# Folding weights loaded in group 5 and folded in group 11 of a four-block kernel, their sums on GpSimd in the attention

## The reference, cut to what matters

```
x = x + _L0_ffn_ref(_L0_cond_ref(x, itok_B_0_15, L0_cond_weights), L0_ffn_qweight, ...)
x = x + _L1_ffn_ref(_L1_cond_ref(x, L1_cond_Wq, L1_cond_Wk, L1_cond_Wv, L1_cond_Wo, ...), ...)
x = x + _L2_ffn_ref(_L2_cond_ref(x, itok_B_0_15, L2_cond_W, L2_cond_lora_A, L2_cond_lora_B), ...)
x = x + _L3_ffn_ref(_L3_cond_ref(x, itok_B_0_7, ...), ...)
```

```
def _qlora_linear(x, wq, A, B):
    w = jnp.tile(wq, (1, 4))
    base = x @ w.T
    lora = x @ A.T @ B.T
    return base + lora * LORA_SCALING
```

## Time and profile before

| | us |
|---|---|
| median of 3 runs | 2923.24 |
| lowest and highest | 2919.52 and 2926.33 |
| the profiled execution | 2924.63 |
| its span | 2922.9 |
| TensorE busy in the span | 2838.4 |
| first stage (first attention row of TensorE) | 101.67 |

### The profile page before, as it was taken

The page is one execution under the profiler, slowest core; times in us unless marked ns, Lnnn a source line. Parts: engine busy times, 40 slices in busy tenths (PEclk is TensorE's granted clock), DMA queues, the critical chain, the costliest instruction groups (busy, mean ns, idle before and its releaser), DMA issues. The chain is left out here.

```text
span 2922.9 us, 56003 instructions
## 1 busy us (share of the span) xinstructions
PE 2838.4 (97%) x14852; PEld 1935.0 (66%) x14852; DVE 1973.4 (68%) x4703; ACT 1140.2 (39%) x2462; POOL 1523.1 (52%) x1465
## 2 busy tenths in 40 slices
PE   6889999999999999999999999999999999999997
PEld 4566666666666666666666666666666667677775
DVE  5566666666666666566666666666666666677776
ACT  3444444444444444344444444444444444122222
POOL 6566666656666666666666666666666663100000
PEclk9999999999999999999999999999999999999998
DMA  8444444444444444544544444444444446412120
GB/s 306 162 124 122 124 124 124 127 127 127 127 127 127 127 127 127 199 123 123 177 125 127 125 123 120 115 122 125 126 124 119 119 125 196 129 45 58 40 48 15
DMA packets 429458, 363.47 MB, mean 124 GB/s; under 512 B 89094, under 2 KB 369690, under 8 KB 428346
## 3 DMA queue, kind: packets, MB, share of 16 engines
q1 hardware_dynamic: 376346, 184.56, 22.5%
q0 software_dynamic: 49136, 169.56, 18.2%
q10 hardware_dynamic: 3888, 8.24, 0.8%
HBM read 335.14 MB, written 18.61 MB: 121 GB/s over the span
## 5 line engine op out<-in xcount | busy, mean ns | idle before, releaser
L549 DVE CUSTOM_DVE_ANT_0 ps_s<-ps_s,mask 128x544 f32<-128x544 f32 x512 | 374.1, 731 | 537.5 <-PE ps_s L393 524.3
L302 POOL DMA_INDIRECT v_sb<-in_v_rows_w,v_row x504 | 488.4, 969 | 460.0 <-PE ps_oT L421 251.2
L361 PE MATMUL ps_t<-wqkv,xT 128*128 128x512 f32 x1488 | 702.5, 594 | 4.6 <-DMA wqkv<-in_wqkv_w 4.6
L465 ACT ACTIVATE ps_s<-ps_s,nmax 128x544 f32<-128x544 f32 x512 | 352.5, 689 | 868.7 <-DVE nmax L549 868.7
L416 PEld LDWEIGHTS ps_oT<-pT,v_sb 128*128 128x128 f32 x4096 | 528.0, 192 | 189.2 <-issue 176.9
L416 PE MATMUL ps_oT<-pT,v_sb 128*128 128x128 f32 x4096 | 542.8, 276 | 9.5 <-DMA v_sb<-in_v_rows_w,v_row 9.5
L374 PE MATMUL ps_t<-wo,oT 128*128 128x512 f32 x992 | 507.8, 594 | 0.0
L392 PE MATMUL ps_s<-k_sb,qkT 128*128 128x416 f32 x1024 | 445.7, 517 | 6.5 <-PEq L715 4.2
L401 PEld LDWEIGHTS ps_pT<-ident_sb,p_sb 128*128 128x128 f32 x2048 | 256.1, 141 | 270.7 <-issue 246.1
L586 DVE STREAM_TRANSPOSE qkT<-rot 32x640 f32<-32x640 f32 x496 | 414.3, 835 | 14.5
L560 DVE TENSOR_SCALAR p_sb<-ps_s,rinv 128x512 f32<-128x512 f32 x512 | 384.5, 751 | 26.8 <-DVE rinv L557 0.3
(11 more groups left out here) (235 smaller groups left out, 3236.0 us busy)
## 6 DMA issues: line engine op xcount, KB each, us to landing
k_sb<-in_kT SPq DMA_DIRECT2D x2048, 64.0 KB
v_sb<-in_v_rows_w,v_row POOLq DMA_INDIRECT x512
wo<-in_wo_w POOLq DMA_DIRECT2D x2, 4096.0 KB, 14.4
v_new<-v_raw SPq DMA_DIRECT2D x512, 16.0 KB, 1.8
xT<-x1T_scratch POOLq DMA_DIRECT2D x31, 256.0 KB, 5.1
y_scratch<-y_sb SPq DMA_DIRECT2D x31, 256.0 KB
wqkv<-in_wqkv_w SPq DMA_DIRECT2D x6, 1024.0 KB, 12.1
wqkv<-in_wqkv_w POOLq DMA_DIRECT2D x6, 1024.0 KB, 13.9
```

What stands on the lines that cost most here:

```text
L302: e.indirect_dma_start(out=v_sb[:, b % 2, c, :], out_offset=None, in_=A["v_rows_w"], in_offset=bass.IndirectOffsetOnAxis(ap=v_row[:, b, c: ...
L361: m = e.matmul(ps_t[bank_of(t)][:, :], xT[:, k, :], wqkv[:, k, 512 * t:512 * t + 512], start=k == 0, stop=k == KC - 1)
L465: e.activation(scores(u), scores(u), ACT.Exp, bias=nmax[:, u % 2:u % 2 + 1], scale=-1.0, accum_out=rsum[:, u % 2:u % 2 + 1]).then_inc(expe ...
L549: e.tensor_tensor_reduce(out=scores(u), in0=scores(u), in1=mask[:, b % 2, :], scale=-SCALE, scalar=3e38, op0=ALU.add, op1=ALU.min, accum_o ...
```

## The change

It does four things. (1) The loads of the five folding weights go from the start of ScalarE's stream to its step 5, ahead of the copy for group 6. (2) The folding products, with ScalarE's copies of them, go from step 3 to step 11; they now wait for the last projection's sum and copy, the first projection no longer waits for the fold, and the first transpose of q (`turn_q`) does. (3) The sums of quarters leave VectorE; GpSimd makes them in the attention, after the memset, as six adds, and issues the two stores itself ahead of its wait for them. (4) The one-column exponential goes from the end of the first stage to the start of ScalarE's attention stream.

```
@@ attention, gpsimd, after the memset of v_new
+            fold, n = inside(wo, FOLD), 0
+            for to, of in (("w2f", "w2"), ("b2f", "b2")):
+                into, part = fold[to][:, :, 0:P], fold[of].rearrange("p k (j n) -> p k j n", j=KC)
+                e.tensor_tensor(into, part[:, :, 0, :], part[:, :, 1, :], ALU.add).then_inc(fold_summed, 1)
+                for j in range(2, KC):
+                    n = n + 1
+                    e.wait_ge(fold_summed, n)
+                    e.tensor_tensor(into, into, part[:, :, j, :], ALU.add).then_inc(fold_summed, 1)
+                n = n + 1
+            e.wait_ge(fold_summed, n)
+            e.dma_start(A["c_w2f"], fold["w2f"]).then_inc(W.out_fold, 16)
+            e.dma_start(A["b2f"].rearrange("(c a) r n -> (a r) c n", c=2), fold["b2f"]).then_inc(W.out_fold, 16)
             e.wait_ge(W.out_fold, 32)
@@ attention, scalar
+            e.activation(W.warm[:, :], W.mhalf[:, 0:1], ACT.Exp)
             exp(0, 0)
@@ embed
-    FOLD_AT = 3
+    FOLD_AT, FOLD_LOAD_AT = 11, 5
-    SUMS_AT = {7: ("w2f", "w2"), 8: ("b2f", "b2")}
@@ embed, sync, at its end
-            e.wait_ge(folded_v, 2)
-            e.wait_ge(folded_a, 2)
-            e.dma_start(A["c_w2f"], fold["w2f"]).then_inc(out_fold, 16)
-            e.dma_start(A["b2f"].rearrange("(c a) r n -> (a r) c n", c=2), fold["b2f"]).then_inc(out_fold, 16)
@@ embed, tensor: fold_down, project(0), turn_q(0)
                 e.wait_ge(dma_fold, 16 * 5)
+                e.wait_ge(W.summed, NQT)
+                e.wait_ge(W.raw_copied, NT)
...
                     e.wait_ge(x1T_copied, 1)
-                    e.wait_ge(folded_a, 2)
...
-                    e.wait_ge(W.summed, NQT)
-                    e.wait_ge(W.raw_copied, NT)
+                    e.wait_ge(folded_a, 2)
@@ embed, scalar
-            e.wait_ge(dma_q, 16 * 5)
-            for name in ("w2t", "b2t", "a13", "w2", "b2"):
-                e.dma_start(fold[name], A["c_" + name]).then_inc(dma_fold, 16)
...
             for g in range(GROUPS):
+                if g == FOLD_LOAD_AT:
+                    for name in ("w2t", "b2t", "a13", "w2", "b2"):
+                        e.dma_start(fold[name], A["c_" + name]).then_inc(dma_fold, 16)
...
-            e.activation(warm[:, :], offs[:, :], ACT.Exp)
@@ embed, vector
-                if g in SUMS_AT:
-                    to, of = SUMS_AT[g]
-                    e.wait_ge(dma_fold, 16 * 5)
-                    e.tensor_reduce(fold[to][:, :, 0:P], fold[of].rearrange("p k (j n) -> p k n j", j=KC), AX.X, ALU.add).then_inc(folded_v, 1)
```

More of the change, by code:

```diff
@@ L72, in __init__ @@
         self.qkT = sb("qkT", [P, GB, HT, S], F32)
+        self.warm = sb("warm", [P, 1], F32)
         self.dma_bt, self.bt_bounded, self.rows_ready, self.half_made = (sem(n) for n in ("dma_bt", "bt_bounded", "rows_ready", "half_made"))
@@ L170, in attention @@
     dma_vn = [sem(f"dma_vn{b}") for b in range(GB)]
-    v_cleared = sem("v_cleared")
+    v_cleared, fold_summed = sem("v_cleared"), sem("fold_summed")
     scored, masked, mask_made, exped = sem("scored"), sem("masked"), sem("mask_made"), sem("exped")
@@ L637, in embed @@
     fold = inside(wo, FOLD)
-    dma_fold, folded_v, turned_down, folded_a = (sem(n) for n in ("a_dma_fold", "a_folded_v", "a_turned_down", "a_folded_a"))
+    dma_fold, turned_down, folded_a = (sem(n) for n in ("a_dma_fold", "a_turned_down", "a_folded_a"))
     k_room, v_room = W.k_sb[:, :, :, :, :].rearrange("p i j h s -> p (i j h s)"), W.v_sb[:, :, :, :].rearrange("p i c n -> p (i c n)")
@@ L671, in embed @@
     invf = sb("invf", [P, HD], F32)
-    warm = sb("warm", [P, 1], F32)
     voff = sb("voff", [P, HALVES], F32)
@@ L691, in embed @@
     dma_x = [sem(f"a_dma_x{i}") for i in range(XB)]
-    out_xT, out_fold = W.out_xT, W.out_fold
+    out_xT = W.out_xT
     out_tab, bd_zero = sem("a_out_tab"), sem("a_bd_zero")
```

## The result

The changed kernel takes 2930.21 us, median of 10 runs (2925.61 to 2938.45), against 2921.36 for the kernel before, also of 10 (2918.91 to 2926.33). The ratio is 1.0030 with a 95% interval of 1.0022 to 1.0039: slower by 8.85 us in the medians, 6.4 to 11.4 by the interval. The prediction was 2929.8; none of its rivals came true. The profiled execution of the changed kernel took 2928.63 us (span 2926.9) beside 2924.63 (2922.9) before.

What follows compares the result with a forecast made beforehand. TensorE, running almost without gaps, was taken as the bound. The terms -1.50 + 0 + 0 + 0.94 + 7.2 = +6.6 us gave 2929.8 us from the median of 2923.24, with an 8 in 10 range of 2921 to 2933.

Steps and rivals of the forecast that it cites:

- The folding loads, +7.2: First stage: the five late loads overtake x of group 7 and delay its mix by 5.5 to 9.0 us, middle +7.2.
- over half the bytes from 43 to 52: Sign, first stage: ScalarE's queue q10 moves over half the DMA bytes from 43 to 52 us.
- x of group 8: First stage: with the full 9.0 us delay it lands at 65.4 and is wanted at 66.4, so in time.
- fold_down at step 11 and the table, +0.94 - 1.50: Late first stage: fold_down adds 5.36, saves 2.66 wait before group 14 and 1.76 slow stretch; table at hand-over saves 1.50.
- The sums on GpSimd, 0: Start of attention: GpSimd's adds, 5.3 us, and stores, some 6, fit rotation's 12.04 us wait; cost 0, bounds 0, +1.
- the rotation of round 1 starting with a wait still above zero: Sign, attention: after 11.3 us of sums and stores GpSimd's first rotation step still waits, out of 12.04 us before.
- the second argument: Attention: even if 5 us late at the rotation's first step, GpSimd waits again for each of the next two sums.
- in any case: First stage: without fold_down at step 3, x of group 7 lands at 51.8 anyway; removal wins 0 of 5.36 us.
- Rival A: First stage: loads do not push x of group 7 back; mix stays at 51.78, sum -0.6, 2922.7 us; chance 0.20.
- B: First stage: x of group 7 comes over 5 us sooner; some 2917 us, faster by over 0.2%; chance 0.05.
- D: Attention: GpSimd's sums delay the rotation of round 1 and TensorE; some +3 beside the rest; chance 0.04.
- C: First stage: ScalarE's x1T stores queue behind the loads, x of groups 8 and 9 late too; +11.4, 2934.6 us; chance 0.09.

Runs made afterwards that it cites:

- e1: The changed kernel with the five folding loads back at the start of ScalarE's stream: 2927.3 us against 2928.01 for the kernel before, ratio 0.9994.
- e4: The changed kernel with the folding loads as thirteen transfers with rows of 2 KB, same step: 2933.68 us against 2928.01 for the kernel before, ratio 1.002.
- e5: The changed kernel with w2 and b2 loaded at the start, the other three (1.84 MB) in step 5: 2929.38 us against 2922.5 before, ratio 1.0023.
- e10: The kernel before, unchanged, profiled a second time: 2930.76 us, one execution.
- e11: The changed kernel, unchanged, profiled a second time: 2933.24 us, one execution.
- e2: The kernel before with only the table's exponential moved into attention: 2926.22 us against 2928.01 for the kernel before, ratio 0.9995.
- e9: The kernel before with only the sums of quarters and their stores moved to GpSimd in attention: 2926.2 us against 2927.88 before, ratio 1.000.
- e6: The changed kernel with folding loads at the start, K pages four steps later, wqkv slices 3 to 5 one later: 2918.07 us against 2922.5 before, ratio 0.9984.
- e7: The kernel before with the table in attention, K pages four steps later, wqkv slices 3 to 5 one later: 2917.86 us against 2922.5, ratio 0.9983.

## Why the prediction was right

The mechanism was the one predicted and carries the result. That 2929.8 lies 0.4 us from the measured 2930.21 is luck: the sum of +6.6 was some 2.2 too small, and the median of before from three runs (2923.24) was 1.9 above that from ten (2921.36).

**The folding loads, +7.2.** Measured +7.87 at the mix of group 7 in the first pair (7.4 without the 0.5 us by which the changed kernel was late already before 28 us, a difference with no place that I could name); at the first attention row the loads alone are 7.27 (e1). The route is the one predicted: the removal of fold_down at step 3 turned into a longer wait, ScalarE issued right behind the store of group 2 (40.09, against "about 40"), q10 had 0.97 of 1.65 MB from 48 to 52 us, and x of group 7 came last. The sign "over half the bytes from 43 to 52" was not quite there: over all of that stretch q10 moved 1.68 of 3.71 MB, since GpSimd's queue q0, with the rows of V, took 1.42 and had been left out of the sharing. Of the two ends, 2.1 MB and all 3.41 MB, the upper one was right: all landed first. By bytes over rate that makes 8.3 us and not 9.0, since the DMA engines moved 409 GB/s there and not 380. So the mis-sized part of this term is the middle, 7.2, taken for want of knowing how much SyncE's queue still held: the upper end, at the rate measured there, would have been nearer. e1 shows that the term is the loads and nothing else; e4 shows the turns by packet. That delay is not simply bytes over rate is seen in e5 (5.5 us for 1.84 MB, 4.5 by the rate).

The Trainium skill, "DMA: Bandwidth & Descriptors" (Queues, rings and completion order), has the rule that a DMA engine goes round its queues one packet at a time. Both traces agree that turns go by packet: 180, 179 and 180 packets with 0.97, 0.60 and 0.08 MB, and with rows of 2 KB 454 and 454 with 0.83 and 0.77. What the profile counts as a packet is no more than one row of a transfer (the pages' come to some 440 bytes each); the Trainium skill's packet holds several descriptors, and no run here shows a turn of that size.

**x of group 8** didn't wait (67.25), as worked out, and everything behind shifted by the same amount.

**fold_down at step 11 and the table, +0.94 - 1.50.** From the mix of group 7 to the first attention row it is 101.67 - 51.78 = 49.89 us before and 108.96 - 59.65 = 49.31 after, -0.58 where -0.56 was predicted. So close an agreement is luck: e1 gives -0.15 for the same stretch, and e10 and e11, where before waits elsewhere, +3.4. What holds is that the wait before group 14 is gone. The table alone is -1.43 by the first attention row and -1.51 by the wait ahead of it (e2). The Trainium skill, "ScalarE: Activation LUTs" (What ACT_TABLE_LOAD costs), adds a drain of 1.38 us to a load of 1.28. The load here is 1.28, the next ACTIVATE starts 1.30 after the load's start, and moving both saved 1.43 to 1.51: the sum by the row was right, and the drain isn't seen. In attention 0.87 of the 3.61 us wait ahead of the first exponential is left. The load and its exponential take 1.5 of that; most of the rest went because the first scores came sooner, at a clock of 1.00 and not 0.50.

**The sums on GpSimd, 0.** Right in the total (e9: ratio 1.000), wrong on the way: "the rotation of round 1 starting with a wait still above zero" failed. The adds took 6.4 us, not 5.3: the nearest row, 1.05 us, was a multiplication by one value for each row, where these add quarters of a wide tile and take 1.30, and which of the differences costs it was not tested. The issue and the landing of the stores ate the rest of the 12.04. What saved the term was the second argument, that GpSimd waits again for each of the next two sums: 1.16 and 3.41 us.

**What was missed.** The clock at the hand-over, worth up to 3 us between two executions (12.23 and 9.31 us to the first product with V), was in no term; the range had 2 us for scatter, taken from three runs. Nor was it seen that x of group 5 can wait from 0.45 to 3.73 us from one execution of the changed kernel to the next, nor that the kernel before, with fold_down in step 3, can lose some 5.5 us ahead of its first projection and then not wait for x of group 7: "in any case" was too strong for a load whose landing at 51.8 was read from one execution. From sum to result: the predicted +6.6, the +7.1 to +7.3 of the first attention row in two pairs, and the medians' +8.85 all lie in the interval of 6.4 to 11.4, so the last 1.6 us have no cause that these runs could show.

Rival A fell with the mix at 59.65, B with it; D with e9. C's mechanism, x of groups 8 and 9 late too, was not there: SyncE's four pages took 13.10 us to issue instead of 8.39, but group 8 was in time.

## What to carry to other kernels

In the stretch from 28 to 52 us the DMA share was at its full (1.04), and there three things held. Work removed from the engine that waits won nothing (e1). A load that was added cost about its bytes over the rate, 8.3 us for 3.41 MB at 409 GB/s, and somewhat more for the half of it (e5). And it cost them to the queue with the smallest packets, even to a load issued earlier. So before moving a load, look for the slices where the DMA share is near 1, and keep it, or move what else stands there, out of them: loading pages later won 4.5 us (e6, e7), which the change itself did not. Look too at more than one execution before taking a row as the place of a wait: the kernel before had two patterns of waits in its first stage. A part that wins 1.5 us at a hand-over is real in the trace and still too small to see in the median.

## What was not expected of the hardware

A load issued 0.15 us ahead of five others on another queue landed 0.5 us after the last of them (59.6 and 59.1). Thirteen issues in that crowd held ScalarE for 7.8 us (44.76 to 52.53), five for 2.95 (40.46 to 43.41), and four page issues held SyncE for 13.10. The clock granted in the first 5 us of attention was anything from 0.50 to 1.00 over thirteen profiles, and differed between executions of one kernel. Its cause is open, as are those of the wait for x of group 5 and of the 5.4 to 5.8 us that three of five profiles with fold_down in step 3 lose ahead of the first projection.
